# Output biases added by accumulating DMAs instead of TensorE products, and a GpSimd product behind one more wait

## The reference

```
n   = layernorm(x)
phi = cumsum((n @ W_omega.T + b_omega) * exp(log_scale) / sqrt(position))
cr, ci = n * cos(phi), n * sin(phi)
mr, mi = cumsum(cr) / position, cumsum(ci) / position
rr, ri = mr*cos(phi) + mi*sin(phi),  mi*cos(phi) - mr*sin(phi)
h   = layernorm(concat(cr, ci, rr, ri)) * gamma + beta        # 1024 wide
h   = gelu(h @ W1.T + b1) @ W2.T + b2                         # 512, then 256 wide
x   = x + n + h
out = x + relu(layernorm(x) @ Wq1.T + f_b1) @ Wq2.T + f_b2    # 1024 wide, ternary weights
```

## Time and profile before

| | before |
|---|---|
| median of 3 runs | 1599.02 us (1599.0 to 1600.2) |
| the profiled execution's own time | 1598.85 us |
| its span | 1597.1 us |
| PE busy | 1524.3 us (95%) |
| DVE busy | 1418.5 us (89%) |
| ACT busy | 1268.4 us (79%) |
| POOL busy | 505.0 us (32%) |
| mean granted TensorE clock | 0.985 |

### The profile page before, as it was taken

One profiled execution on the slowest core, in us unless ns is written; L12 is line 12 of the kernel. 1 busy time (PEld: TensorE's weight loads), 2 busy tenths in 40 slices (PEclk: granted clock), 3 DMA queues, 4 the chain that ended last, 5 costly groups with the idle time before them and its releaser, 6 DMA issues.

```text
span 1597.1 us, 30622 instructions
## 1 busy us (share of the span) xinstructions
PE 1524.3 (95%) x11177; PEld 932.7 (58%) x11177; DVE 1418.5 (89%) x2304; ACT 1268.4 (79%) x1805; POOL 505.0 (32%) x331
## 2 busy tenths in 40 slices
PE   3789999999999999999999999999999999999994
PEld 2455556666655666665566666556666556666662
DVE  7999999999999999999998999999999999999832
ACT  6768878888987888897788788878888887887743
POOL 1222333323233333223333322333332233333310
PEclk9799999999999999999999999999999999999997
DMA  5212332332333333233233323323323332332313
GB/s 204 54 40 57 77 70 63 69 79 53 67 80 67 67 67 80 54 67 80 63 68 70 67 68 67 80 54 74 73 59 75 67 80 54 73 61 56 65 27 53
DMA packets 135300, 109.73 MB, mean 69 GB/s; under 512 B 74992, under 2 KB 125424, under 8 KB 135152
## 3 DMA queue, kind: packets, MB, share of 16 engines
q0 software_dynamic: 26112, 50.34, 18.7%
q1 hardware_dynamic: 107408, 53.77, 11.8%
q10 hardware_dynamic: 1632, 3.67, 0.6%
HBM read 23.87 MB, written 33.55 MB: 36 GB/s over the span
## 4 chain that ended last, share of the span: by engine, by line
PE 57%; DVE 22%; issue 9%; ACT 9%; SPq 1%; DMA 1%; DVEq 0%; POOL 0%; POOLq 0%; ACTq 0%
PE ps L881 16%; PE ps L896 11%; PE ps L912 11%; PE ps L931 10%; PE ps L841 5%; DVE mr L1161 4%; DVE ph L1119 3%; ACT base L549 2%; DVE arena L1226 2%; ACT xs L566 2%; DVE bn L1245 2%; DVE mi L1180 1%; SPq L440 1%; DVE rows L1262 1%; DVE rr L1192 1%
## 5 line engine op out<-in xcount | busy, mean ns | idle before, releaser
L881 PE MATMUL ps<-arena,w_hi 128*128 128x512 f16 x2048 | 610.0, 379 | 1.6 <-DVE arena L1202 1.4
L881 PE MATMUL ps<-arena,w_lo 128*128 128x512 f16 x1024 | 388.6, 379 | 0.0
L881 PEld LDWEIGHTS ps<-arena,w_hi 128*128 128x128 f16 x2048 | 198.2, 98 | 223.3 <-issue 3.2
L896 PE MATMUL ps<-turned,fw_t 128*128 128x512 f16 x1024 | 257.7, 381 | 20.1 <-DMA turned<-rows 16.8
L912 PE MATMUL ps<-fw_t,arena 128*128 128x256 f16 x2048 | 254.9, 273 | 0.4 <-DVE arena L1270 0.4
L912 PEld LDWEIGHTS ps<-fw_t,arena 128*128 128x128 f16 x2048 | 200.2, 98 | 57.6 <-issue 5.9
L504 POOL TENSOR_TENSOR sqr<-sqr,turn 128x1024 f32<-128x1024 f32 x32 | 88.3, 2760 | 379.4 <-ACT sqr L613 365.1
L660 ACT ACTIVATE arena<-ps,relu_bias,relu_scale 128x512 f32<-128x512 f32 x256 | 191.9, 773 | 13.8 <-PE ps L896 13.4
L1270 DVE TENSOR_TENSOR arena<-arena 128x512 f16<-128x512 f32 x256 | 170.8, 688 | 28.4 <-ACT arena L669 22.4
L931 PE MATMUL ps<-w_hi,arena 128*128 128x256 f16 x1024 | 183.4, 273 | 0.0
L881 PEld LDWEIGHTS ps<-arena,w_lo 128*128 128x128 f16 x1024 | 100.2, 98 | 121.2 <-issue 0.7
(11 more groups left out here) (192 smaller groups left out, 2894.8 us busy)
## 6 DMA issues: line engine op xcount, KB each, us to landing
x_rows<-in_L_attn_x SPq DMA_DIRECT2D x32, 512.0 KB, 4.2
rr<-qa POOLq DMA_DIRECT2D x32, 512.0 KB, 4.5
ri<-qb POOLq DMA_DIRECT2D x32, 512.0 KB, 4.4
out<-x SPq DMA_DIRECT2D x32, 512.0 KB, 2.9
out<-x POOLq DMA_DIRECT2D x32, 512.0 KB, 6.2
arena<-in_L_attn_W ACTq DMA_DIRECT2D x1, 2048.0 KB, 11.0
arena<-in_L_ffn_W SPq DMA_DIRECT2D x2, 1024.0 KB, 11.3
turned<-rows SPq DMA_TRANSPOSE x128, 2.4
```

Of the source, the lines that this page charges most:

```text
L881: last = pe.matmul(ps[:, 4 + m], w[:, k, m * P:(m + 1) * P], a[:, c.b, k], start=(i == 0), stop=(i == len(passes) - 1))
L896: last = pe.matmul(ps[:, 4 + m % KE], fw1_t[:, k, m * P:(m + 1) * P], a[:, k], start=(i == 0), stop=(i == len(passes) - 1))
```

## The change

The eight bias products of a step, `bias_row` and all that makes it are gone. In their place POOL issues two accumulating DMAs in each step, between `inverse_std_1(far)` and `inverse_std_context(nxt)`:

- `base_bias(ahead)` adds `b2`, read from DRAM as one row of 1 KB for each of 128 partitions x 4 groups, to `base[ahead]` after `base_scaled(ahead)`; `mixer_residual` of the next step waits for it.
- `x1_bias(now)` adds `f_b2` in the same form to `x1[now]` after `normalise_2(now)` has read it. SP's store of `x1[now]` waits for it (before: for `x1_done`).

Apart from this, `product_imag_sin` on POOL also waits for `sumr_done`, the end of the real scans of its chunk, and the semaphores of the feed-forward blocks are one each instead of one for each of four slots; the values waited for stand for the same events.

```diff
+        b2_rows = b2.partition_broadcast(P).unsqueeze(1).to_broadcast([P, NT, D])
+        f_b2_rows = f_b2.partition_broadcast(P).unsqueeze(1).to_broadcast([P, NT, D])
@@ SP
                 if c := s.chunk(0):
-                    need(sp, x1_done, c)
+                    need_dma(sp, x1_biased, c)
                     sp.dma_start(out_v[c.index], x1[:, c.b]).then_inc(stored[c.b], 16)
@@ POOL
+            def base_bias(c):
+                need(pool, scaled_done, c)
+                pool.dma_start(base[:, c.b], b2_rows, accum_op=ALU.add).then_inc(base_biased[c.b], 16)
+
+            def x1_bias(c):
+                need(pool, xs2_done, c)
+                pool.dma_start(x1[:, c.b], f_b2_rows, accum_op=ALU.add).then_inc(x1_biased[c.b], 16)
@@
                 if far:
                     inverse_std_1(far)
+                if ahead:
+                    base_bias(ahead)
+                if now:
+                    x1_bias(now)
                 if nxt:
                     inverse_std_context(nxt)
@@
             def product_imag_sin(c):
                 need(pool, mi_done, c)
                 need(pool, sin_done, c)
+                need(pool, sumr_done, c)
@@ PE, ffn_out
-                    for j in range(NT):
-                        pe.matmul(ps_rows_a[:, j], ones_h[:, :], bias_row[:, 1], start=(j % 2 == 0), stop=False,
-                                  skip_group_check=True)
...
-                                         start=False, stop=(m == KF - 1 and a is rl),
+                                         start=(m == 0 and j % 2 == 0 and a is rh), stop=(m == KF - 1 and a is rl),
@@ PE, mixer_out
-                    pe.matmul(ps_rows_b[:, j], ones_h[:, :], bias_row[:, 0], start=True, stop=False)
...
-                                         start=False, stop=(i == len(passes) - 1))
+                                         start=(i == 0), stop=(i == len(passes) - 1))
@@ DVE, mixer_residual
-                need(dve, scaled_done, c)
+                need_dma(dve, base_biased, c)
@@ DVE, step -1
-                    bias_pieces()
```

More of the change, by code:

```diff
@@ L249, in phase_mixer_layer @@
         added = [sem(f"added{i}") for i in range(2)]
+        base_biased = [sem(f"base_biased{i}") for i in range(2)]
+        x1_biased = [sem(f"x1_biased{i}") for i in range(2)]
         bn1_done, mv1_done, ve1_done = sem("bn1_done"), sem("mv1_done"), sem("ve1_done")
@@ L281, in phase_mixer_layer @@
         turn2_begun, turned2_done = sem("turn2_begun"), sem("turned2_done")
[L283 to L287, removed]
+        f1_done = sem("f1_done")
+        relu_done = sem("relu_done")
+        rh_done = sem("rh_done")
+        rl_done = sem("rl_done")
+        f2_done = sem("f2_done")
         out_done = sem("out_done")
@@ L345, in need_turned, with need_block @@
             wait(eng, turned2_done, c.counts.value(16 * NT, 16 * NT * (c.more + 1 - back)))
-        def need_block(eng, sems, m, c, back=0):
-            wait(eng, sems[m % SLOTS], c.counts.value(2, 2 * (c.more - back) + m // SLOTS + 1))
+        def need_block(eng, s, m, c, back=0):
+            wait(eng, s, c.counts.value(KF, KF * (c.more - back) + m + 1))
         def stand_alone(eng):
@@ L372, in phase_mixer_layer @@
         W2_GROUPS = range(1 + KC, 1 + KC + KE // 2)
-        BIAS_GROUP = 1 + KC + KE // 2
-        groups.append(([(bias_cols, i, 0) for i in range(2 * KD)],
-                       bias_row[:, :, :].rearrange("p i d -> p (i d)"), None, None))
+        FIRST_SIGNS = 1 + KC + KE // 2
         for k in range(KD):
@@ L382, in phase_mixer_layer @@
                            fw2_t[:, k:k + 2, :].rearrange("p k e -> p (k e)"), None, None))
[L383 to L387, removed]
+        SIGN_GROUPS = range(FIRST_SIGNS, len(groups))
+        FW1_TURNED = FIRST_SIGNS + 2 * KD
+        group_banks = [0] + [(1, 4, 5, 6, 0)[n % 5] for n in range(KC)] + [0, 1]
+        group_banks += [n % 2 for n in range(len(SIGN_GROUPS))]
         def group_out(eng, n):
@@ L392, in group_out @@
                 eng.wait_ge(p_wo_lo, 1)
-            elif n < BIAS_GROUP:
+            elif n < FIRST_SIGNS:
                 eng.wait_ge(p_lo, n)
             else:
-                eng.wait_ge(p_plain, n - BIAS_GROUP + 1)
+                eng.wait_ge(p_plain, n - FIRST_SIGNS + 1)
         def first_chunks(eng):
@@ L530, in _ @@
             square_sums(first)
+            base_bias(first)
             prepared(pool)
@@ L660, in relu @@
                 act.activation(rf[:, m % SLOTS], ps[:, 4 + m % KE], ACT.Relu, scale=relu_scale[:, 0:1],
-                               bias=relu_bias[:, m:m + 1]).then_inc(relu_done[m % SLOTS], 1)
+                               bias=relu_bias[:, m:m + 1]).then_inc(relu_done, 1)
             def relu_hi(c, m):
@@ L668, in relu_hi @@
                     need_block(act, f2_done, m + SLOTS, c, 1)
-                act.copy(rh[:, m % SLOTS], rf[:, m % SLOTS]).then_inc(rh_done[m % SLOTS], 1)
+                act.copy(rh[:, m % SLOTS], rf[:, m % SLOTS]).then_inc(rh_done, 1)
             def step(s):
@@ L689, in step @@
                         group_lo(n)
-                    group_hi(BIAS_GROUP)
                 if now:
@@ L888, in ffn_in @@
                     if isinstance(c.index, int) and c.index == 0:
-                        pe.wait_ge(p_plain, 1 + len(SIGN_GROUPS))
+                        pe.wait_ge(p_plain, len(SIGN_GROUPS))
                 if m >= KE:
@@ L897, in ffn_in @@
                                      start=(i == 0), stop=(i == len(passes) - 1))
-                last.then_inc(f1_done[m % SLOTS], 1)
+                last.then_inc(f1_done, 1)
             def ffn_out(c, m):
@@ L912, in ffn_out @@
                         last = pe.matmul(ps_rows_a[:, j], a[:, m % SLOTS, j * P:(j + 1) * P], fw2_t[:, m],
-                                         start=False, stop=(m == KF - 1 and a is rl),
+                                         start=(m == 0 and j % 2 == 0 and a is rh), stop=(m == KF - 1 and a is rl),
                                          skip_group_check=True)
-                last.then_inc(f2_done[m % SLOTS], 1)
+                last.then_inc(f2_done, 1)
             def mixer_out(c, before):
@@ L980, in turn_group @@
                     pe.wait_ge(p_fold, KE)
-                elif scale == 2:
+                else:
                     pe.wait_ge(p_w2, 16)
-                else:
-                    pe.wait_ge(p_cols, 1)
                 bank_free(n)
@@ L1270, in relu_lo @@
                 dve.tensor_tensor(rl[:, m % SLOTS], rf[:, m % SLOTS], rh[:, m % SLOTS], ALU.subtract)\
-                   .then_inc(rl_done[m % SLOTS], 1)
+                   .then_inc(rl_done, 1)
             def step(s):
@@ L1367, in powers @@
                 return dve.tensor_scalar(down[:, cols], pw[:, cols], 2.0 ** -14, None, ALU.mult)
[L1369 to L1382, removed]
             def signs(i, w, into):
@@ L1446, in _ @@
             beta_dot(3)
-            dve.wait_ge(p_vec, 64)
+            dve.wait_ge(p_vec, 32)
             link(dve.tensor_tensor(b1_full[:, :], b1_dot[:, :], b1_raw[:, :], ALU.add))
```

14 lines of the change are left out of this document (1 added, 13 removed).

## The result

| | before | after |
|---|---|---|
| median | 1599.01 us (4 runs) | 1937.68 us (1933.41 to 1942.12, 4 runs) |
| ratio, 95% interval | | 1.2115 (1.2097 to 1.2134) |
| span of the profiled execution | 1597.1 us | 1940.3 us |
| PE busy | 95% | 80% |
| mean granted clock | 0.985 | 0.908 |

The kernel became 339 us slower; 1682 us (1600 to 1746) was forecast. The direction and the place were right; the loss was four times the one forecast.

The account below looks back on a forecast made before the run. PE's work (46.80 us a step) and a ring through the transposes (46.62) were taken as bounds. From 1598.85 us, less 2.5 for the prologue, plus 81 for the 49.5 us ring and 5 for the tail: 1682 us, range 1600 to 1746.

Parts of the forecast that it names:

- the place and the mechanism: In SP's stream the store waits for x1_bias with the transposes behind it; +2.7 us a step, +81 us in 30 steps.
- the removed products: On PE between L896 and L1110, eight bias products a step go: 0.88 us a step, 28.2 us in all.
- prologue: Before the steps, bias_pieces' 11 small DVE operations go: 2.5 us gained, bounds 0 to 3.
- base's DMA: base_bias on POOL's queue: its landing is hidden, but it is issued ahead of x1_bias, taking 1.34 us to issue.
- the term for `x1_bias`'s landing: From x1_bias's issue on POOL to its landing: 7.6 us, bounds 5.8 (like L465) and 8.8 (like L472).
- the term for the transposes: Four transposes' issue and landing, 6.27 us, plus 0.5 us for store and load ahead of them on the queue.
- the clock as a rival of its own: PE's gap each step also lowers the granted clock: 1708 us, or 1733 if in all steps; chance 0.13.
- The first piece of the ring: On PE, from a step's first L896 to the first L1110: 21.59 us before, 20.71 us after the change.
- the ring: Chain through the transposes, PE, DVE, ACT and back: 46.62 us a step before, 49.5 after, between 47.25 and 51.5.
- to the end of `xs2`: From the first L1110 to the end of normalise_2, DVE and ACT without slack: 11.85 us.
- to the issue of `x1_bias`: On POOL, from the end of xs2 to the issue of x1_bias, behind L460 and base_bias's issue: 1.76 us.
- nothing for the GpSimd product's wait: POOL's product behind the real scans: DVE gains 1.4 to 2.1 us a step, costed at nothing for the time.

Follow-up runs that it names:

- Run 2: Changed kernel with SP's four transposes put before the store and the load, bias DMAs unchanged; 1623.3 us, ratio 1.0154 to the kernel before.
- Run 1: Changed kernel without base_bias and x1_bias, the store waiting for x1 as before; 1561.44 us, ratio 0.9756.
- run 3: Kernel before with one line added: the GpSimd product also waits for the real scans; 1590.41 us, ratio 0.9940.
- run 4: Changed kernel with base's bias alone, x1's left out and the store waiting for x1 as before; 1564.93 us, ratio 0.9783.
- run 5: Changed kernel without base_bias, so with the bias of x1 alone; 1800.64 us, ratio 1.1256.
- run 6: Changed kernel with both new DMAs reading the chunk's 512 distinct rows of x in DRAM instead of one row; 1762.09 us, ratio 1.1024.
- run 7: Changed kernel with both new DMAs reading f_b2 from SBUF, one row in each partition; 1751.36 us, ratio 1.0943.
- run 12: Changed kernel with the bias of x1 alone, read from a row in each partition of SBUF; 1593.69 us, ratio 0.9963.
- Run 8: Changed kernel with rr's accumulating DMA on GpSimd issued only when the transposes have landed; 1845.33 us, ratio 1.1532.
- run 11: Changed kernel with the bias row in SBUF plus 18 extra PE products before the wait for the transposes; 1734.78 us, ratio 1.0863.
- Run 10: Changed kernel with 36 extra products on PE in front of the wait for the transposes; 1907.76 us, ratio 1.1945.
- run 13: Changed kernel with SP's transposes before store and load, and both bias DMAs behind GpSimd's retrieval DMAs; 1569.68 us, ratio 0.9812.
- run 9: Changed kernel with SP's load of x_rows behind the transposes, the store still in front; 1884.93 us, ratio 1.1778.

## Why the prediction was wrong

**Right: the place and the mechanism.** The store's wait for `x1_bias` holds the transposes behind it in SP's stream, and PE has no slack there. Run 2 shows it: the same DMAs, another order, 314 us less.

**Right: the removed products.** 28.2 us forecast. Run 1 gained 38.2 us against its own kernel before, of which run 3 gives the GpSimd wait 9.3. That leaves 29 us for products and prologue, 30.7 forecast.

**Right: base's DMA costs next to nothing by itself** (run 4, 3.5 us), **but it delays x1's** (run 5: 9.3 instead of 12.0 us of landing).

**Wrong: the term for `x1_bias`'s landing, 7.6 us.** It measured 12.0, and 12.1 up to the store on average over 27 steps. I bounded it by L465 and L472 and took 8.8 us for the upper end. Neither of these reads one row of DRAM many times, so their rows are no bound for one that does. With distinct rows the landing is 8.3 us (run 6), inside my bounds. By the Trainium skill's formula for a DMA issued by GpSimd (DMA: Bandwidth & Descriptors, Anatomy of one DMA — SWDGE path) 512 KB take an estimated 3.2 us. The traces disagree for accumulating ones: the shortest median landing is 4.4 us (L468, before), and 5.9 us for a bias (runs 7 and 12).

**Wrong: the term for the transposes, 6.27 + 0.5 us.** It measured 9.54 in the step shown and 9.6 on average. I had priced store and load in front of them, and nothing for the accumulating DMA of rr, because in the kernel before it starts when they have landed. Once the transposes are later by more than a few us they fall on it. Run 8 takes this collision away and gains 92 us; the stretch is then 6.9 us, as forecast, with store and load still in front. The delay follows the time at which rr's DMA is issued after the first transpose (means of 27 steps): 9.6 us where it is issued 0.9 us after; 7.7 to 8.5 where it is 4.4 to 4.8 (runs 5, 6, 7, 11); 6.9 and 7.1 where it is 7.1 and 7.9 (runs 8 and 12).

**Wrong: the clock as a rival of its own (0.13).** My forecast had a gap of 3.6 us; the two errors above made it 10 us, and then the fall was no longer a matter of chance. Run 10 gained 30 us, 1.4 us a step, with a filler that held the clock in part of the steps. The first piece of the ring takes 20.3 us where the clock never falls (runs 1, 12, 13) and 22.4 in the changed kernel, so the fall costs 2.1 us a step (the forecast's 20.71 was 0.4 too long). The price of 1.7 us a gap was about right; what was wrong is the assumption that the clock stays at 1.00.

The pieces of the ring, as means of 27 full steps read from the timelines (us):

| | forecast | changed | run 8 | run 10 | run 11 |
|---|---|---|---|---|---|
| first transpose to first product | 6.82 | 9.61 | 6.87 | 9.49 | 8.02 |
| to the phase turns | 20.71 | 22.37 | 22.06 | 21.33 | 20.65 |
| to the end of `xs2` | 11.85 | 11.77 | 11.77 | 11.77 | 11.77 |
| to the issue of `x1_bias` | 1.76 | 1.16 | 1.16 | 1.16 | 1.16 |
| to the store | 7.6 | 12.13 | 11.91 | 11.89 | 8.38 |
| to the next first transpose | 0.80 | 1.10 | 1.10 | 1.10 | 1.15 |
| sum | 49.5 | 58.1 | 54.9 | 56.7 | 51.1 |

Of the excess of 8.6 us in the changed kernel, landing makes half (4.5), the collision a third (2.8) and the clock most of the rest (1.7). The three feed each other, so the single runs do not add up: removing the slow row alone (runs 6 and 7) gave 176 and 186 us, more than its own 4 us a step, since part of the collision and about half of the gap went with it.

**Wrong: nothing for the GpSimd product's wait.** I looked only at the ring through the transposes, where L1161 does not lie. But L1226 comes behind it, and the feed-forward products need L1226's result before they may overwrite its bank. Before, PE's weight loads waited 15.9 us for it, in 26 waits; in run 3, 0.7 us. The step fell from 46.80 to 46.55 us, and 0.23 of that lies between the first product and the phase turns, where those weight loads are. That the wait was worth 9.3 us is measured; that these waits are the whole of it is an inference.

**What is left in run 11:** it has 51.2 us a step where the prediction's ring with the landing measured there (8.4) gives 50.3. The transposes' stretch accounts for it: 8.0 us for 6.8. Run 8 has the same store and load in front of the transposes and takes 6.9, so it is not these: it is rr's DMA, which still comes before the transposes have landed.

**Still open:** why 512 reads of one row of DRAM are slow, and how much of run 9's gain is the load itself and how much the later rr.

## What to carry to other kernels

A wait added to a queue is paid by what stands behind it in that queue: here a store that nobody needed soon had four transposes behind it on which everything depended. Put the urgent transfer first, and the one that can wait behind the transfers that are waited for; the same two DMAs then cost 8 us instead of 376. Do not bound an unknown DMA by rows that differ from it in the one property that is new, and when a stall moves a transfer by several us, look at what else is in flight at its new time.

## What the runs showed of the hardware

- An accumulating DMA of 512 KB into SBUF in packets of 1 KB landed in 9.3 us when all packets read the same 1 KB of DRAM, in 6.3 us from distinct rows of DRAM, and in 5.9 us from a row in each partition of SBUF (runs 5, 6 and 7). A second one issued right behind landed 12.0, 8.3 and 8.1 us after its issue.
- Four transposing DMAs took 5.12 us to issue and landed in 2.4 us (medians, kernel before); 5.6 and 3.2 us directly behind 1 MB of store and load (run 8); 7.7 and 5.6 us with an accumulating DMA between SBUF tensors in flight as well (changed kernel), whose own landing went from 4.5 to 6.8 us; and 6.2 and 5.5 us, with the store and the load behind them, beside accumulating DMAs from DRAM into SBUF (run 2).
- A gap of 10 us on PE in each step brought the clock to 0.50 in each, for 4 us or more after work resumed: eight products took 3.25 to 3.60 us instead of 1.90. With 18 or 36 unneeded products in the gap they took 1.90 in 21 of 27 and in 10 of 24 steps (the mean clock of the span was 0.98 and 0.97).
- Two scans beside a GpSimd multiplication took 2.1 us longer (4.44 and 2.39 us a pair, the kernel before and run 3); placed after the scans, the multiplication delays the next operation with two SBUF inputs, by 0.5 us on average in run 3, and not the one in between that reads PSUM (677 and 683 ns).
